# Low halves of the first graph sum's features: from one DVE operation each to two POOL operations each

## What is computed

```python
def _L0_gnn_ref(x, edge_index, W, b):
    n = x.shape[0]
    self_loops = jnp.arange(n, dtype=edge_index.dtype)
    src = jnp.concatenate([edge_index[0], self_loops])
    dst = jnp.concatenate([edge_index[1], self_loops])
    deg = jax.ops.segment_sum(jnp.ones_like(dst, dtype=x.dtype), dst, num_segments=n)
    dinv = jnp.where(deg > 0, jax.lax.rsqrt(deg), 0.0)
    norm = dinv[src] * dinv[dst]
    xw = x @ W
    msgs = xw[src] * norm[:, None]
    agg = jax.ops.segment_sum(msgs, dst, num_segments=n)
    return jax.nn.relu(agg + b)
...
x = x + _L0_gnn_ref(_layernorm(x, axis=-1), edge_index, L0_gnn_W, L0_gnn_b)
```

## Time and profile before

| | |
|---|---|
| median of 3 runs | 1409.96 us (1409.1 to 1410.52) |
| profiled execution, its own time | 1410.52 us |
| its span | 1408.8 us |
| busy PE / PEld / DVE / ACT / POOL | 1272.6 / 887.0 / 611.3 / 398.8 / 206.4 us |
| low halves (L1059), DVE | 25 operations, 493 ns median each |

### The profile page before, as it was taken

The page is one execution under the profiler, slowest core; times in us unless marked ns, Lnnn a source line. Parts: engine busy times, 40 slices in busy tenths (PEclk is TensorE's granted clock), DMA queues, the critical chain, the costliest instruction groups (busy, mean ns, idle before and its releaser), DMA issues. The chain is left out here.

```text
span 1408.8 us, 20986 instructions
## 1 busy us (share of the span) xinstructions
PE 1272.6 (90%) x8083; PEld 887.0 (63%) x8083; DVE 611.3 (43%) x1515; ACT 398.8 (28%) x948; POOL 206.4 (15%) x206
## 2 busy tenths in 40 slices
PE   4757999997998999999999999999999817999993
PEld 4654777774554764446777644457777616888883
DVE  7689777734775451311333342232322271222221
ACT  3556666624774230100000000100222301222220
POOL 3200000001322000000000000000000003777772
PEclk9956999998999999999999999999999857999997
DMA  7102322331000314556565444568654253766665
GB/s 217 47 2 99 110 72 73 117 118 40 1 1 1 119 41 147 159 145 155 126 140 122 136 134 147 161 154 188 147 119 92 61 189 102 162 148 145 161 148 132
DMA packets 259896, 161.29 MB, mean 114 GB/s; under 512 B 171680, under 2 KB 248895, under 8 KB 259599
## 3 DMA queue, kind: packets, MB, share of 16 engines
q1 hardware_dynamic: 248878, 144.64, 37.0%
q0 software_dynamic: 10912, 15.24, 6.3%
HBM read 84.23 MB, written 41.08 MB: 89 GB/s over the span
## 5 line engine op out<-in xcount | busy, mean ns | idle before, releaser
L855 PE MATMUL bank<-weights,agg_in_out 128*128 128x320 f16 x2000 | 274.8, 299 | 0.0
L869 PE MATMUL bank<-weights 128*128 128x512 f16 x1250 | 270.3, 379 | 1.1 <-issue 1.1
L855 PEld LDWEIGHTS bank<-weights,agg_in_out 128*128 128x128 f16 x2000 | 195.7, 98 | 76.2
L869 PEld LDWEIGHTS bank<-weights 128*128 128x128 f16 x1250 | 122.3, 98 | 148.5 <-issue 1.5
L1023 PE MATMUL bank<-weights,agg_in_out 128*128 128x320 f16 x1000 | 162.1, 300 | 0.1
L687 POOL TENSOR_TENSOR shift<-shift,rstd 128x5 f32<-128x5 f32 x15 | 3.6, 243 | 942.5 <-ACT rstd L692 942.5
L1000 ACT CAST weights<-bank 128x500 f16<-128x500 f32 x160 | 114.0, 722 | 77.8 <-PE bank L989 77.8
L1023 PEld LDWEIGHTS bank<-weights,agg_in_out 128*128 128x128 f16 x1000 | 92.5, 98 | 28.4 <-ACT weights L1000 0.4
L2093 PE MATMUL bank<-wk,weights 128*128 128x256 f32 (+1 forms) x512 | 105.2, 360 | 0.9 <-DVE wk L2139 0.9
L2108 PE MATMUL bank<-weights 128*128 x448 | 105.4, 384 | 0.5 <-ACT weights L2124 0.2
L1651 DVE SCALAR_TENSOR_TENSOR wk<-bank,inverse_degree,wk 128x256 f32<-128x256 f32 x50 | 24.0, 480 | 181.6 <-ACT wk L1843 181.6
(11 more groups left out here) (359 smaller groups left out, 1471.5 us busy)
## 6 DMA issues: line engine op xcount, KB each, us to landing
weights<-counts_source_target SPq DMA_DIRECT2D x50, 800.0 KB, 4.6
counts_source_target<-weights SPq DMA_DIRECT2D x5, 4000.0 KB, 13.3
weights<-in_L_ffn_W SPq DMA_DIRECT2D x32, 512.0 KB, 4.1
weights<-in_L_ffn_W SPq DMA_DIRECT2D x4, 1024.0 KB, 6.0
rows_and_gates<-normed SPq DMA_DIRECT2D x1, 3300.0 KB, 12.0
token_out<-residual SPq DMA_DIRECT2D x1, 3200.0 KB, 19.6
edge_windows<-edges_packed SPq DMA_DIRECT2D x1, 3129.0 KB
out<-token_out SPq DMA_DIRECT2D x1, 3120.0 KB
```

What stands on the lines that cost most here:

```text
L855: last = nc.tensor.matmul(bank, source[:, 5 * k + c, part * F + fh * P:part * F + fh * P + P], MB[:, k, c, h * HALF:(h + 1) * HALF], start ...
L869: last = nc.tensor.matmul(ps[j][:, :], MB[:, k, c, j * P:(j + 1) * P], source[:, 5 * k + c, :], start=(k == 0 and c == 0), stop=(k == 4 an ...
```

## The change

The DVE loop loses its low halves. POOL makes them at the start of its part of the block: for five row tiles it scales `Z` in place by `dinvf`, waits for that to be written (new semaphore `rows_scaled`), and then subtracts the high halves into the low columns. The counter that PE waits for is the same. `Z` is not read again before the next layer norm overwrites it, behind POOL's later products.

```diff
-        st2 = tally("windows_stored")
+        st2, z_sc = tally("windows_stored"), tally("rows_scaled")
...
-        def low_half_dve(group):
+        def low_half_pool(pool, group):
             for c in range(5 * group, 5 * group + 5):
-                last = nc.vector.scalar_tensor_tensor(XH2[:, c, F:2 * F], Z[:, c, 0:F], dinvf[:, c:c + 1],
-                                                      XH2[:, c, 0:F], ALU.mult, ALU.subtract)
+                last = pool.tensor_scalar(Z[:, c, 0:F], Z[:, c, 0:F], dinvf[:, c:c + 1], 1.0, ALU.mult, ALU.mult)
+            last.then_inc(z_sc.sem, 1)
+            pool.wait_ge(z_sc.sem, z_sc.at(group + 1))
+            for c in range(5 * group, 5 * group + 5):
+                last = pool.tensor_tensor(XH2[:, c, F:2 * F], Z[:, c, 0:F], XH2[:, c, 0:F], ALU.subtract)
             last.then_inc(a_in.sem, 1)
...
-                            if b < 0 and s % 6 == 5:
-                                low_half_dve(s // 6)
...
                 with pool.Else():
+                    for g in range(5):
+                        low_half_pool(pool, g)
                     for g in range(5):
                         normalise_pool(pool, l2_rt, l2_sc, g)
```

## The result

The changed kernel takes 1414.82 us (median of 6 runs, 1413.03 to 1416.72) against 1410.2 us before (median of 6, 1408.77 to 1412.17). The ratio is 1.0029, with a 95% interval of 1.0019 to 1.0039: slower by 4.6 us, where 9.5 were forecast. The sign, the place and the engines are those of the prediction; the size is half.

The account below looks back on a forecast made before the run. DVE was taken to bound the block's first stage, PE those behind it. Turns with POOL make the stage 40.7 us against 31.2, +9.5 us, so 1409.96 becomes 1419.5 us; range 1412 to 1430.

Parts of the forecast that it names:

- What bounds the kernel: Block's first stage: DVE sets its 31.2 us; removing the 9.9 us of low halves alone moves first sum to 120.4.
- The cause: Stage before the first sum: DVE comparisons and POOL operations take turns, one waiting until the other has moved its data.
- the sum for the turns: First stage: POOL's 50 operations alternate with 50 comparisons, 36.0 us, plus 4.7 alone: 40.7 against 31.2, +9.5 us; chance 0.66.
- the slope of the affine select: Price of POOL's scaling from its nearest one-input row: 0.92 ns an element, 0.24 us of data, about 0.41 in all.
- the 512-element product: Price of POOL's subtraction from a two-input row, 1272 ns for 512 elements: 0.54 us of data, 0.74 in all.
- lower bound of +6.5 us: First stage, turns with each comparison counting only its own data, 0.27 us: stage 37.7 us, +6.5.
- 1415 to 1428 given for this case: Whole-kernel range in us for the likeliest case, DVE and POOL taking turns, centred forecast 1419.5; chance 0.66.
- rival of two comparisons for each POOL operation: First stage 33.8 us, +2.6; POOL ends late, PE waits 0.4 to 6 us: +3 to +9, about 1416; chance 0.12.
- DVE's casts: Profile evidence for one-for-one turns: beside two casts, 1.99 us together, POOL's affine selects start 1.02 apart instead of 0.25.
- PE waiting for POOL: First quarter of the sum: denied, since POOL is done at about 134 and the first sum starts at about 139.8.
- No contention: Rival: first stage takes 21.3 us, POOL undisturbed ends at 125.3; gain 9.9 us, 1400.1; chance 0.12.
- Holding for the whole instruction: Rival: in the first stage each engine waits out the other's fixed part too; stage 50.0 us, +18.8, 1428.8; chance 0.10.

Follow-up runs that it names:

- The runs with one kind alone: Changed kernel with low columns zeroed beforehand and POOL making scalings only, 1405.66 us; with subtractions only, of unscaled rows, 1412.95 us; kernel before 1411.03 us.
- the two changed lengths: POOL making only ten double-length scalings, 1403.57 us against 1410.6 before; only 25 half-length unscaled subtractions, 1403.98 us against 1409.45 before.
- the memsets: Scalings-only version with each scaling replaced by a 128x256 POOL memset that reads nothing: 1400.78 us against 1411.03 for the kernel before.

## Why the prediction was off

**What bounds the kernel: right.** DVE sets the stage and nothing stands close behind it: without the halves the first sum comes at 120.41 (forecast 120.4) and the run is 10.0 us shorter (9.9, with an interval of some 6.5 to 11).

**The cause: right.** A comparison and a POOL operation that reads exclude each other, and the comparison is held for the data part of the latter. The runs with one kind alone, the two changed lengths and the memsets show it.

**Where it failed: the sum for the turns**, "POOL's 50 operations go with 50 comparisons in 25 x (0.57 + 0.87) = 36.0 us". It charged the stage with 25 x 0.24 + 25 x 0.54 = 19.5 us of holds; the stage got 13.9, namely 22 scalings at 0.20 (4.4) and 20 subtractions at 0.475 (9.5). Two parts make up the 5.6 us:

- The data of both were taken too long, the scaling's by 0.04 us (0.24 from the slope of the affine select, 0.20 measured), the subtraction's by 0.065 (0.54 from the 512-element product, 0.475 measured): 25 x 0.04 + 25 x 0.065 = 2.6 us.
- One scaling takes two comparisons, not one. That costs DVE nothing by itself, but POOL falls behind: its work would need 75 comparisons and the stage has 64. The last two scalings and five subtractions, 2.8 us of holds, slip into the next stage, where PE sets the pace and DVE has slack. The very first scaling (0.2 us) starts ahead of DVE and holds nothing. Together these are 3.0 us.

So 21.3 + 13.9 = 35.2 us for the stage, as measured, 4.0 more than before. That is also below the prediction's own lower bound of +6.5 us, and 1414.82 lies just outside the 1415 to 1428 given for this case. The bound let the comparison shrink to 0.27, which it did not do, kept the subtraction's 0.54, and kept one comparison for each of the 50 operations. The prediction had the second part as its rival of two comparisons for each POOL operation, with 3 to 9 us, but set it against the turns for all 50 operations; what the runs show is one for the subtractions, two for the scalings. That 4.6 us lies in this rival's span is luck: its time came from PE waiting for the last halves, and PE did not wait. It took the one-for-one rhythm from POOL operations beside DVE's casts, which last about 1 us each. Both the form and the length are other there than in the stage, and which of the two makes the difference is not shown. The row was read beyond its reach.

**PE waiting for POOL: rightly denied**, though for a wrong time: POOL ended at 138.3, not 134, and the fifth group's slack carried it (the first sum was at 134.25 and its part at 142.19).

**Not foreseen:** 0.4 us in the first quarter from a clock that rose later, for a reason that stays open.

**The rivals.** No contention fell with the first row of the profile. Holding for the whole instruction fell too: a scaling, 0.48 us long where DVE has not begun yet (the shortest of the 25), holds a comparison for 0.20, a subtraction, 0.67 us long there (in the run with subtractions only), for 0.475. The Trainium skill (SBUF — State Buffer, "Who interferes with whom") has an exclusive lock there, which the prediction took to the letter as this rival; the measured holds are shorter than the whole instruction, and the measurement decides.

## What to carry over

Moving work from a saturated engine to an idle one pays only if the idle one's work does not hold the saturated one. Here a row tile cost DVE 0.394 us when it did the work itself and 0.20 + 0.475 = 0.675 us in holds when POOL did it, so nothing was gained by it in a stage where DVE never rests. Groups put on POOL for the next stage, where holds cost nothing, were not tried. First look for gaps of the busy engine itself, in the block before and in the next stage: those gave 6.3 us, by filling two waits and by making two groups nearer to when they are needed.

## What the runs showed that I had not expected

- Two-input comparisons of 0.333 us on DVE beside a queue of one-input POOL operations settle into a fixed rhythm, two comparisons for each, for lengths of 256 and 512 elements; beside two-input POOL operations they go one for one, for 256 and 128. The reason was not found.
- A POOL operation that only writes (0.31 us memsets) takes nothing from a two-input DVE comparison, while a one-input operation of DVE (L359) lost 1.00 us to a memset.
- Work that delays a stage can slip out of it: of 16.9 us of holds (25 x 0.20 + 25 x 0.475) 2.8 fell in the next stage, where they cost nothing, and 0.2 ahead of the first comparison, which is why the whole change costs 4.0 us in the stage and not 7.0.
